# Layer 2 edge norm: folding ln_g into the weights, one vector operation in place of two and a wide maximum

## The reference, cut to what matters

```
src, dst = edge_indices
edge_inputs = concat([x[src], x[dst], edge_features], axis=1)       # 128 + 128 + 64
h = edge_inputs @ W1 + b1
h = (h - mean(h)) * rsqrt(var(h) + 1e-5) * ln_g + ln_b
h = relu(h)
messages = (h @ W2 + b2) * sigmoid(edge_features @ gate_w + gate_b)
agg = segment_sum(messages, dst)
gi = agg @ W_ih.T + b_ih
gh = x @ W_hh.T + b_hh
...                                                                  # GRU cell of gi, gh and x
```

## Time and profile before

| | us |
|---|---|
| runs | 5134.09, 5176.93, 5184.84 |
| median | 5176.93 |
| span of the profiled execution | 5142.6 |
| second layer, first gather to the end | 2646.6 to 5142.6 |
| TensorE busy | 3506.5 (68%) |
| VectorE busy | 4015.9 (78%) |
| ScalarE busy | 2380.6 (46%) |
| GpSimd busy | 3316.3 (64%) |

### The profile page before, as it was taken

One profiled execution on the slowest core, in us unless ns is written; L12 is line 12 of the kernel. 1 busy time (PEld: TensorE's weight loads), 2 busy tenths in 40 slices (PEclk: granted clock), 3 DMA queues, 4 the chain that ended last, 5 costly groups with the idle time before them and its releaser, 6 DMA issues. The chain is left out here.

```text
span 5142.6 us, 108062 instructions
## 1 busy us (share of the span) xinstructions
PE 3506.5 (68%) x20734; PEld 3121.8 (61%) x20735; DVE 4015.9 (78%) x15806; ACT 2380.6 (46%) x6569; POOL 3316.3 (64%) x3375
## 2 busy tenths in 40 slices
PE   5543666666666666666547877777777777777776
PEld 4432555656665565655547767666666666666665
DVE  8995677777777777777758988877877877877876
ACT  2211233333333333333336665665665655665654
POOL 0004777777777777777747777666666666666661
PEclk9655677776767777678868898888889888898887
DMA  3113445555555554555444444333333333333331
GB/s 105 45 35 92 130 139 145 145 142 145 145 142 144 146 145 142 143 144 145 142 107 106 108 110 105 97 96 98 94 96 100 96 92 100 95 95 100 98 94 40
DMA packets 597657, 576.83 MB, mean 112 GB/s; under 512 B 320530, under 2 KB 462744, under 8 KB 597312
## 3 DMA queue, kind: packets, MB, share of 16 engines
q0 software_dynamic: 133952, 329.07, 23.6%
q1 hardware_dynamic: 463360, 244.62, 17.8%
HBM read 536.53 MB, written 43.09 MB: 113 GB/s over the span
## 5 line engine op out<-in xcount | busy, mean ns | idle before, releaser
L1662 POOL DMA_INDIRECT crows<-c,gather_index x1664 | 1666.9, 1002 | 738.8 <-issue 469.7
L1187 POOL DMA_INDIRECT bxrows<-bx,gather_index x1664 | 1620.0, 974 | 507.5 <-issue 506.0
L1222 PE MATMUL scattered<-bxrows,hotw 128*128 128x129 f32 x3328 | 695.2, 378 | 552.7 <-DVE hotw L1385 552.0
L1222 PEld LDWEIGHTS scattered<-bxrows,hotw 128*128 128x128 f32 x3328 | 604.7, 272 | 634.5 <-DVE acc L1382 553.9
L1710 PE MATMUL scattered<-z,hotw 128*128 128x129 f32 x3328 | 560.1, 336 | 503.3 <-DVE hotw L1912 503.2
L1710 PEld LDWEIGHTS scattered<-z,hotw 128*128 128x128 f32 x3328 | 518.3, 242 | 534.8 <-issue 489.5
L1891 DVE SCALAR_TENSOR_TENSOR z<-h,rstd,ln_g 128x128 f32<-128x128 f32 x1664 | 577.6, 347 | 237.8 <-issue 237.5
L1212 PE MATMUL pre<-near,hotT 128*128 x3328 | 595.1, 352 | 211.2 <-DVE h L1360 177.8
L1695 PE MATMUL pre<-w1e,efT 128*128 128x129 f32 x3328 | 691.6, 291 | 66.8 <-DVE h L1883 34.0
L1382 DVE TENSOR_TENSOR acc<-acc,scattered 128x129 f32 x1664 | 471.2, 283 | 326.2 <-ACT mask L1293 320.6
L1212 PEld LDWEIGHTS pre<-near,hotT 128*128 128x128 f32 x3328 | 558.1, 260 | 261.2 <-issue 257.9
(11 more groups left out here) (268 smaller groups left out, 5599.5 us busy)
## 6 DMA issues: line engine op xcount, KB each, us to landing
spread<-place_rows SPq DMA_DIRECT2D x416, 256.0 KB, 3.5
ef<-in_edge_attr SPq DMA_DIRECT2D x1664, 32.0 KB
bxrows<-bx,gather_index POOLq DMA_INDIRECT x1664
crows<-c,gather_index POOLq DMA_INDIRECT x1664
x_turned<-x1T SPq DMA_DIRECT2D x98, 64.0 KB
g_xT<-x_turned SPq DMA_DIRECT2D x98, 64.0 KB
x_a<-in_x SPq DMA_DIRECT2D x97, 64.0 KB
x_b<-in_x SPq DMA_DIRECT2D x97, 64.0 KB
```

The costliest lines, as they stand in the source:

```text
L1187: pool.indirect_dma_start(out=bx[q][:, k, 0:2 * D], out_offset=None, in_=s.bx[:, :], in_offset=bass.IndirectOffsetOnAxis(ap=s.index[:, g * ...
L1222: last = nc.tensor.matmul(out[:, k // 2, k % 2, 0:W], hotw[v % 2][:, k, :], bx[v][:, k, D:D + W], start=True, stop=True)
L1662: pool.indirect_dma_start(out=crows[q][:, k, 0:D], out_offset=None, in_=s.c[:, :], in_offset=bass.IndirectOffsetOnAxis(ap=s.index[:, g * G ...
```

## The change

The scale `ln_g` leaves the loop. With |g| the size and s the sign of `ln_g`, relu(g*a + b) = |g| * (max(s*a, -b/|g|) + b/|g|). The sign goes into the columns of the centred W1 and of the bias (`sign_g`, in `centre`), so `h` already carries it. The size goes into the rows of the product of W2 and W_ih, when it is copied out (`size_g`, in `copy_folded`). What is left for the loop is `z = max(h * rstd, floor_b)` with `floor_b = -ln_b / |g|`, one operation for each chunk, and the 512-wide maximum is gone. PE now waits for the semaphore of that operation itself (`z_made`; `scaled` is gone). Sizes are kept above 1e-30.

The early part gets two more DMAs, four small operations on DVE, and its subtractions become operations with two tensors. The start of the second layer gets a chain of four operations on DVE, `floor_b`, in place of one negation.

```diff
     def load(sp):
 ...
+        sp.dma_start(ln_g[:, :], ins["L1_gnn_ln_g"].rearrange("(d a) -> d a", a=1)).then_inc(w_in, 16)
+        sp.dma_start(sign_g[:, :], row("L1_gnn_ln_g").to_broadcast([P, D])).then_inc(w_in, 16)
 ...
     def turn_weights(pe):
-        pe.wait_ge(w_in, 16 * 11)
+        pe.wait_ge(w_in, 16 * 13)
 ...
     def centre(dve):
-        dve.wait_ge(w_in, 16 * 11)
+        dve.wait_ge(w_in, 16 * 13)
+        dve.tensor_scalar(sign_g[:, :], sign_g[:, :], 0.0, 2.0, ALU.is_ge, ALU.mult).then_inc(chain, 1)
+        dve.scalar_tensor_tensor(size_g[:, :], ln_g[:, :], -1.0, ln_g[:, :], ALU.mult, ALU.max).then_inc(chain, 1)
         dve.reduce_sum(total[:, :], raw[:, :, :], axis=mybir.AxisListType.X).then_inc(chain, 1)
-        dve.wait_ge(chain, 1)
+        dve.wait_ge(chain, 3)
         dve.tensor_scalar(mean[:, :], total[:, :], 1.0 / D, None, ALU.mult).then_inc(chain, 1)
-        dve.wait_ge(chain, 2)
+        dve.tensor_scalar(sign_g[:, :], sign_g[:, :], -1.0, None, ALU.add).then_inc(chain, 1)
+        dve.tensor_scalar(size_g[:, :], size_g[:, :], LEAST, None, ALU.max).then_inc(chain, 1)
+        dve.wait_ge(chain, 6)
         for j in range(2):
-            dve.tensor_scalar(s.w1cd[:, j * D:(j + 1) * D], raw[:, j, :], mean[:, j:j + 1], None, ALU.subtract)
 ...
+            dve.scalar_tensor_tensor(s.w1cd[:, j * D:(j + 1) * D], raw[:, j, :], mean[:, j:j + 1], sign_g[:, :],
+                                     ALU.subtract, ALU.mult)
 ...
     def copy_folded(dve):
         dve.wait_ge(folded, 1)
-        dve.tensor_copy(fold[:, :], m_ps[:, :, :].rearrange("p j d -> p (j d)")).then_inc(rows_done, 1)
+        dve.tensor_scalar(fold[:, :], m_ps[:, :, :].rearrange("p j d -> p (j d)"), size_g[:, 0:1], None,
+                          ALU.mult).then_inc(rows_done, 1)
 ...
             def _(act):
-                act.wait_ge(negated, 2)
+                act.wait_ge(negated, 1)
 ...
-                            act.wait_ge(scaled, g * 2 - 4)
+                            act.wait_ge(z_made, g * 2 - 4)
 ...
             def _(dve):
-                dve.tensor_scalar(neg_b[:, :], neg_b[:, :], -1.0, None, ALU.mult).then_inc(negated, 1)
                 dve.tensor_scalar(gb[:, :], gb[:, :], -1.0, None, ALU.mult).then_inc(negated, 1)
-                dve.wait_ge(negated, 2)
+                dve.scalar_tensor_tensor(size_g[:, :], size_g[:, :], -1.0, size_g[:, :],
+                                         ALU.mult, ALU.max).then_inc(floored, 1)
+                dve.wait_ge(floored, 1)
+                dve.tensor_scalar(size_g[:, :], size_g[:, :], LEAST, None, ALU.max).then_inc(floored, 1)
+                dve.wait_ge(floored, 2)
+                dve.reciprocal(size_g[:, :], size_g[:, :]).then_inc(floored, 1)
+                dve.wait_ge(floored, 3)
+                dve.scalar_tensor_tensor(floor_b[:, :], floor_b[:, :], -1.0, size_g[:, :],
+                                         ALU.mult, ALU.mult).then_inc(floored, 1)
+                dve.wait_ge(floored, 4)
 ...
                             last = dve.scalar_tensor_tensor(z[par][:, k, 0:D], h[par][:, k, 0:D],
-                                                            rstd[:, par, k:k + 1], ln_g[:, :], ALU.mult, ALU.mult)
+                                                            rstd[:, par, k:k + 1], floor_b[:, :], ALU.mult, ALU.max)
                             if k % 4 == 3:
-                                last.then_inc(scaled, 1)
+                                last.then_inc(z_made, 1)
 ...
-                        if has(g, 2) and k % 4 == 3:
-                            half = k // 4
-                            dve.wait_ge(scaled, g * 2 + half - 3)
-                            part = z[par][:, 4 * half:4 * half + 4, 0:D]
-                            dve.tensor_tensor(part, part, spread_b, ALU.max).then_inc(z_made, 1)
```

More of the change, by code:

```diff
@@ L50 @@
 PAD = BASE | (LOW << 14)
+LEAST = 1e-30
 assert N <= LOW and BODIES * R * G == STEPS and WIDE == STEPS and REST % P == 64 and UNITS == 13
@@ L138, in weights_work @@
     w2T, wihT = sb("w2T", [P, D], F32), sb("wihT", [P, 3 * D], F32)
-    ln_b, b2 = sb("ln_b_col", [P, 1], F32), sb("b2_col", [P, 1], F32)
+    ln_b, b2, size_g = sb("ln_b_col", [P, 1], F32), sb("b2_col", [P, 1], F32), sb("ln_g_size", [P, 1], F32)
+    ln_g, sign_g = sb("ln_g_col", [P, 1], F32), sb("ln_g_sign", [P, D], F32)
     u = sb("u", [P, 1], F32)
@@ L194, in centre @@
     def centre(dve):
-        dve.wait_ge(w_in, 16 * 11)
+        dve.wait_ge(w_in, 16 * 13)
+        dve.tensor_scalar(sign_g[:, :], sign_g[:, :], 0.0, 2.0, ALU.is_ge, ALU.mult).then_inc(chain, 1)
+        dve.scalar_tensor_tensor(size_g[:, :], ln_g[:, :], -1.0, ln_g[:, :], ALU.mult, ALU.max).then_inc(chain, 1)
         dve.reduce_sum(total[:, :], raw[:, :, :], axis=mybir.AxisListType.X).then_inc(chain, 1)
-        dve.wait_ge(chain, 1)
+        dve.wait_ge(chain, 3)
         dve.tensor_scalar(mean[:, :], total[:, :], 1.0 / D, None, ALU.mult).then_inc(chain, 1)
-        dve.wait_ge(chain, 2)
+        dve.tensor_scalar(sign_g[:, :], sign_g[:, :], -1.0, None, ALU.add).then_inc(chain, 1)
+        dve.tensor_scalar(size_g[:, :], size_g[:, :], LEAST, None, ALU.max).then_inc(chain, 1)
+        dve.wait_ge(chain, 6)
         for j in range(2):
-            dve.tensor_scalar(s.w1cd[:, j * D:(j + 1) * D], raw[:, j, :], mean[:, j:j + 1], None, ALU.subtract)
-        dve.tensor_scalar(s.w1e[:, :], raw[0:DE, 2, :], mean[0:DE, 2:3], None, ALU.subtract)
-        dve.tensor_scalar(long[:, 9 * D:10 * D], raw[0:1, 3, :], mean[0:1, 3:4], None, ALU.subtract)
+            dve.scalar_tensor_tensor(s.w1cd[:, j * D:(j + 1) * D], raw[:, j, :], mean[:, j:j + 1], sign_g[:, :],
+                                     ALU.subtract, ALU.mult)
+        dve.scalar_tensor_tensor(s.w1e[:, :], raw[0:DE, 2, :], mean[0:DE, 2:3], sign_g[0:DE, :],
+                                 ALU.subtract, ALU.mult)
+        dve.scalar_tensor_tensor(long[:, 9 * D:10 * D], raw[0:1, 3, :], mean[0:1, 3:4], sign_g[0:1, :],
+                                 ALU.subtract, ALU.mult)
     def copy_turned(dve):
@@ L1505, in layer1_stage @@
         eg, eg1, gate = (sb(n, [P, 2, G], F32) for n in ("eg", "eg1", "gate"))
-        ln_g, neg_b, gb, eps = (
-            sb(n, [P, w], F32) for n, w in (("ln_g", D), ("neg_b", D), ("neg_gate_b", 1), ("eps1", 1)))
+        size_g, floor_b, gb, eps = (
+            sb(n, [P, w], F32) for n, w in (("size_g", D), ("floor_b", D), ("neg_gate_b", 1), ("eps1", 1)))
         efT_ps = ps("efT_ps", [P, G // 2, P], F32)
@@ L1530, in layer1_stage @@
         w_in, zeroed, steps_in, negated = sem("w1_in"), sem("zeroed1"), sem("steps1_in"), sem("negated")
+        floored = sem("floored")
         index_in = sem("index_in")
@@ L1538, in layer1_stage @@
         eg1_made, gates_made, hotw_made = sem("eg1_made"), sem("gates_made"), sem("hotw1_made")
-        scaled, z_made = sem("z_scaled"), sem("z_made")
+        z_made = sem("z_made")
         scattered, added = sem("scattered1_up"), sem("added1")
@@ L1565, in _ @@
                 row = lambda name, n: ins[name].rearrange("(a d) -> a d", a=1).to_broadcast([P, n])
-                sp.dma_start(ln_g[:, :], row("L1_gnn_ln_g", D)).then_inc(w_in, 16)
-                sp.dma_start(neg_b[:, :], row("L1_gnn_ln_b", D)).then_inc(w_in, 16)
+                sp.dma_start(size_g[:, :], row("L1_gnn_ln_g", D)).then_inc(w_in, 16)
+                sp.dma_start(floor_b[:, :], row("L1_gnn_ln_b", D)).then_inc(w_in, 16)
                 sp.dma_start(gb[:, :], row("L1_gnn_gate_b", 1)).then_inc(w_in, 16)
@@ L1861, in _ @@
                 dve.wait_ge(steps_in, 64)
-                dve.tensor_scalar(neg_b[:, :], neg_b[:, :], -1.0, None, ALU.mult).then_inc(negated, 1)
                 dve.tensor_scalar(gb[:, :], gb[:, :], -1.0, None, ALU.mult).then_inc(negated, 1)
-                dve.wait_ge(negated, 2)
+                dve.scalar_tensor_tensor(size_g[:, :], size_g[:, :], -1.0, size_g[:, :],
[8 more added lines that the diff above has]
+                dve.wait_ge(floored, 4)
                 dve.wait_ge(zeroed, R + 3)
-                spread_b = neg_b[:, :].rearrange("p (a d) -> p a d", a=1).to_broadcast([P, 4, D])
                 def steps(g, q, o):
@@ L1874, in steps @@
                         if used(g, 3):
-                            dve.wait_ge(scaled, g * 2 - 4)
+                            dve.wait_ge(z_made, g * 2 - 4)
                             dve.wait_ge(ss_made, g * 2 - 4)
```

## The result

The changed kernel takes 4862.91 us (median of four runs, 4855.03 to 4872.75) against 5178.77 us of the kernel before on the same chip: ratio 0.9431, 95% interval 0.9381 to 0.9481. 4981 us was forecast, with a range down to 4909, so it is faster than the range allows.

What follows compares the result with a forecast made beforehand. VectorE was taken to bound the second layer's loop, GpSimd next. Maxima -206.4 and -2.4, TensorE +11, early part +1.4 gave -196.4 us, off the median 5176.9 to 4980.5, forecast 4981 us, range 4909 to 5049.

Steps and rivals of the forecast that it cites:

- That gap stays.: Second layer's loop: VectorE's 3.60 us of doing nothing before a body's first `h` was to remain after the change.
- What is late next is again VectorE: Second layer's loop: VectorE still sets the pace after the change, 43.07 us a body against GpSimd's 41.6.
- the floor of 41.6 us: GpSimd's gathers in the second layer: 10.39 us a group, so no body of four groups goes below 41.6 us.
- 270 us before now: GpSimd's last gather: could end at 4807 us at the earliest, claimed to be 270 us sooner than in the kernel before.
- The maxima: Second layer's loop: two maxima removed per group, 0.60 us of path time each, 206.4 us over 172 slots.
- The fused `z`: Second layer, VectorE: `z` with maximum as second operation keeps its 347 ns, a change of nothing.
- The 36 slots ahead of the loop: Start of the second layer: gathers set the pace up to about group 27, so no gain was counted there.
- The early part: Before the sort: added small operations and two-tensor subtractions on VectorE cost about 1.4 us, all on the path.
- The first `h`: Start of the second layer: four added operations hide in a 17.88 us wait; start within 2 us of 2673.85 us.
- TensorE's slack: Second layer's loop: shorter slots leave TensorE less time for `pre`; 11 us lost, at most 71 us.
- the rival that was given 0.17: Second layer: TensorE takes over, every body waits as at worst, 71 us lost, gain 136 us, 5041 us; chance 0.17.
- The sum: Whole span: -206.4 - 2.4 + 11 + 1.4 = -196.4 us, a span of 4946 us in place of 5142.6.

Runs made afterwards that it cites:

- b24_shift: Kernel before, maxima still there, with 24 increments of an unused semaphore on VectorE ahead of the second layer's slots: 4967.97 us, ratio 0.963.
- a56_shift: Changed kernel with 56 increments of an unused semaphore on VectorE ahead of the second layer's slots: 5005.69 us, ratio 0.9704 to the kernel before.
- a184_period: Changed kernel with 184 increments of an unused semaphore on VectorE ahead of the second layer's slots: 4986.75 us (one run).
- a45_edge: Changed kernel with 45 increments of an unused semaphore on VectorE ahead of the second layer's slots: 4859.68 us (one run).
- a51_edge: Changed kernel with 51 increments of an unused semaphore on VectorE ahead of the second layer's slots: 4973.90 us (one run).
- al_longer: Changed kernel with four increments of an unused semaphore in each slot of VectorE's loops, main loop 289 instructions again: 4864.24 us (one run).

## Why the prediction was wrong

**The step that failed** is the sentence on the 3.60 us ahead of a body's first `h`: "That gap stays." It was taken for a fixed price of the jump. It was a fetch of code, and it depended on the addresses of the loop: with 53 instructions fewer ahead of the loop and 16 fewer in it (counted in the built programs), its start and its end moved, into three packets. The gap and its twin ahead of the first `z` cost 4.83 us a body (47.87 to 43.04 in `b24_shift`), 208 us over the loop, as much as the maxima; the sum had them at nothing. Where the gap does stay, in `a56_shift`, the ratio is 0.9704, inside the forecast's range (up to 5049 / 5176.9 = 0.975). Three signs stood in the profile of before and were not read: the label "issue" on a wait of 3.60 us where the next slot shows 0.20; the 2.45 us ahead of the `z` that follows; and the 307 packets of q14, 225 of them in the 43 bodies.

The Trainium skill names the mechanism (Runtime: NRT & Kernel Launch, section "Instruction fetch mechanics"): a taken branch to a target outside the two resident blocks of code must wait for a DMA, and its blocks have 16 KiB, 256 instructions. The runs agree that the place of a loop's code can cost such waits, 4.83 us a body here. The size differs: by two blocks of 256 instructions `a56_shift` and `a184_period`, half a block apart, would not both lie badly, and they do, with packets of 8.2 KB. The measurement decides.

**"What is late next is again VectorE"** failed with it. Without the stalls VectorE needs 38.10 us, so the floor of 41.6 us that the prediction had worked out from the earlier trace rows took over (41.52). That floor was right, and right for the end too (4807 us forecast for the last gather, 4806 found); only "270 us before now" is off, as the last gather of the kernel before ends at 5048.4 us, 241 later. Of 47.87 - 38.10 = 9.77 us that VectorE gained, the gathers gave back 3.4.

**The maxima** were sized right: 0.60 us of path time forecast, 0.595 measured. The Trainium skill (VectorE: DVE Perf Modes, section "The DRAIN you can't avoid") says that the next operation waits until the pipeline is empty, and by that alone each would give back 684 ns, 5.5 us a body, which the runs don't bear out. But the same section adds that a next operation which is not held starts earlier, which the prediction left out; the 0.60 us from a maximum's start to the next `z` agree with the addition, so the page does not go against that row.

**The fused `z`**: 347 ns forecast, 349 found (page of the changed kernel). **The 36 slots ahead of the loop**: no gain forecast; from the first `h` to that of group 35 they take 346.9 us against 348.4. **The early part**: `centre` runs from 28.81 to 31.17 us, before from 29.23 to 30.93, so 0.66 us more; 1.4 was forecast. **The first `h`**: 3.81 us later, outside the 2 us that the prediction allowed it.

**TensorE's slack**: 11 us forecast, none found, and not for the reason given: the gathers took the pace, and the clock of 0.53, taken as given, went with the stalls. Where the stalls stay, as the prediction assumed, `h` waits 1.5 us x 43 = 64 us (`a56_shift`). That is near the 71 of the rival that was given 0.17, so that 11 lies near the zero found is luck.

**The sum.** The span was to change by -196.4 us and changed by -271.7, 75.3 more. The loop gives -77.7 of that (1.55 us x 43, and the 11 us for TensorE that were not due), the later start of the second layer +2.4 (2677.66 against 2673.85 us, where 1.4 was forecast); what is left is under 1 us. The other 42 us of the miss are in the base: the median of before lay 32.4 us above its profiled execution (span and 1.9 us around it), the profiled execution after 9.8 us above its median. The first of these is told at the end; the second stays open.

## What to carry to other kernels

An "issue" wait of microseconds at a loop's start, or in the same place of every body, is a question, not a price: look at the instruction queue's packets, and compare with the same operation elsewhere in the loop. Any edit that changes the number of instructions moves all later code of that engine; before its time is put down to what it does, run the old kernel with a few idle instructions ahead of the loop. And when a bound is removed, compare the next engine's floor with what *all* the idle time in the body could give back, also the part that the change isn't aimed at.

## What the runs showed of the hardware that was not expected

- VectorE's loop: free where, by the count above, it touched three 8.2 KB packets of code; about 5 packets fetched per body and 4.8 us lost where it touched four (`b24_shift`, `a45_edge`, `a51_edge`); up to 6.3 us where TensorE's clock fell with it (`a56_shift` 44.38 against VectorE's 38.10).
- Behind an idle stretch of about 5 us TensorE's granted clock was 0.50 for some 10 us of work (the body of `a56_shift` shown). Not every body fell so low; from 3213 to 4650 us the mean was 0.87 in place of the changed kernel's 0.95.
- The traced executions, one of each kernel, fall into two groups some 34 us apart ahead of the second layer, whether changed or not: its first `h` starts at 2674 to 2678 us or at 2708 to 2712 us. The times of the kernel before, at 5131 to 5150 or at 5167 to 5185, fit that, so medians of few runs can differ by as much; the periods of the bodies don't follow it (`a184_period` 44.27 in the one group, `a56_shift` 44.38 in the other). The groups part in the sort, at one wait of VectorE for ScalarE, which copies TensorE's node products out before it comes to that step (kernel before and `b24_shift`, 80 to 135 us). TensorE is equally busy from 40 to 90 us but gets through 247 matmuls in the one group and 142 in the other, while the granted clock is recorded as 1.00 in both (windows: PE busy, PEclk, DMA share, GB/s). What makes TensorE slower there was not tried and stays open.

```profile
DVE keys_odd L297 <- ACT lower_halves L360: 8.0, 1, 8.0
...
40.00:90.00 50.00, 43.77 (x247) 1.00 0.44 122
```
```profile
DVE keys_odd L297 <- ACT lower_halves L360: 43.2, 1, 43.2
...
40.00:90.00 50.00, 43.97 (x142) 1.00 0.24 66
```

- The gathers' pace itself differs between the four versions that it holds up, from 40.66 (`al_longer`) to 41.52 us a body (the changed kernel). Whether the build or the execution makes the difference stays open.
